# A decoder layer in float32 on one core: query projections by one level of Strassen's algorithm

## The reference

```python
q = (hidden_states @ Wq.T).reshape(bsz, q_len, H, HD).transpose(0, 2, 1, 3)
k, v = cross_attention_states @ Wk.T, cross_attention_states @ Wv.T
q, k = _rmsnorm(q, q_norm_w), _rmsnorm(k, k_norm_w)
scores = jnp.einsum('bhqd,bhkd->bhqk', q, k) / np.sqrt(HD) + attention_mask
probs = jax.nn.softmax(scores, axis=-1)
out = jnp.einsum('bhqk,bhkd->bhqd', probs, v)
return out @ Wo.T
```

## Time and profile before

| | |
|---|---|
| median of 3 runs | 1005.98 us |
| lowest, highest | 1003.19, 1006.21 us |
| the profiled execution, own time | 1007.58 us |
| its span, first to last instruction | 1005.8 us |
| mean granted TensorE clock | 0.986 of full |
| PE busy | 966.1 us (96%) |
| DVE, ACT, POOL busy | 573.8, 494.2, 404.0 us |
| HBM traffic | 43.10 MB read, 2.10 MB written |

### The profile page before, as it was taken

The page is one execution under the profiler, slowest core; times in us unless marked ns, Lnnn a source line. Parts: engine busy times, 40 slices in busy tenths (PEclk is TensorE's granted clock), DMA queues, the critical chain, the costliest instruction groups (busy, mean ns, idle before and its releaser), DMA issues.

```text
span 1005.8 us, 15353 instructions
## 1 busy us (share of the span) xinstructions
PE 966.1 (96%) x5010; PEld 804.8 (80%) x5010; DVE 573.8 (57%) x1340; ACT 494.2 (49%) x1368; POOL 404.0 (40%) x341
## 2 busy tenths in 40 slices
PE   5999799999999999899999999999999999999895
PEld 3866488878888888788888888888888888888782
DVE  3665554422321357566666666666566666666777
ACT  4655342422231246555654654654655555555554
POOL 4334634744443453342442442532622623514322
PEclk9999999999999999899999999999999999999997
DMA  6200013310111111011010020020020020100002
GB/s 218 82 3 31 12 46 125 105 63 0 63 63 63 44 62 56 22 43 43 22 54 29 21 83 0 21 83 0 21 83 0 27 78 0 63 0 0 1 1 85
DMA packets 12977, 45.60 MB, mean 45 GB/s; under 512 B 1617, under 2 KB 2257, under 8 KB 9873
## 3 DMA queue, kind: packets, MB, share of 16 engines
q1 hardware_dynamic: 12944, 45.20, 12.9%
HBM read 43.10 MB, written 2.10 MB: 45 GB/s over the span
## 4 chain that ended last, share of the span: by engine, by line
PE 86%; DVE 5%; POOL 3%; ACT 2%; issue 2%; DMA 1%; SPq 0%; POOLq 0%; DVEq 0%; ACTq 0%
PE bank L376 25%; PE bank L378 24%; PE bank L377 24%; PE bank L654 6%; PE bank L664 3%; PE bank L387 1%; POOL res L1438 1%; DVE cbuf L1638 1%; POOL rstd L1333 1%; PE bank L641 1%; DVE bst L1775 1%; POOL h_lo L1327 1%; DMA res<-in_x 1%; PE bank L455 1%; PE bank L744 0%
## 5 line engine op out<-in xcount | busy, mean ns | idle before, releaser
L376 PE MATMUL bank<-act_hi,w_hi 128*128 128x512 f32 x560 | 225.0, 402 | 2.0 <-DVE act_lo L1585 1.6
L378 PE MATMUL bank<-act_hi,w_lo 128*128 128x512 f32 x560 | 220.0, 393 | 0.0
L377 PE MATMUL bank<-act_lo,w_hi 128*128 128x512 f32 x560 | 220.0, 393 | 0.0
L1509 POOL TENSOR_TENSOR pb<-pb,prec 128x512 f32<-128x512 f32 x64 | 66.6, 1040 | 311.6 <-DVE prec L1910 311.6
L1161 ACT ACTIVATE pb<-pb,nmax 128x128 f32<-128x128 f32 x256 | 99.8, 391 | 79.1 <-DVE nmax L1905 79.1
L376 PEld LDWEIGHTS bank<-act_hi,w_hi 128*128 128x128 f32 x560 | 106.1, 189 | 25.6 <-issue 4.3
L378 PEld LDWEIGHTS bank<-act_hi,w_lo 128*128 128x128 f32 x560 | 106.1, 189 | 22.9
L377 PEld LDWEIGHTS bank<-act_lo,w_hi 128*128 128x128 f32 x560 | 106.2, 190 | 22.7 <-issue 1.4
L376 PE MATMUL bank<-w_hi,ot_hi 128*128 128x512 f32 x256 | 105.0, 410 | 0.8 <-DVE ot_lo L1585 0.8
L378 PE MATMUL bank<-w_hi,ot_lo 128*128 128x512 f32 x256 | 100.9, 394 | 0.0
L377 PE MATMUL bank<-w_lo,ot_hi 128*128 128x512 f32 x256 | 100.3, 392 | 0.0
(11 more groups left out here) (190 smaller groups left out, 2066.4 us busy)
## 6 DMA issues: line engine op xcount, KB each, us to landing
raw_a<-in_w_q SPq DMA_DIRECT2D x8, 1024.0 KB, 4.8
raw_b<-in_w_o SPq DMA_DIRECT2D x8, 1024.0 KB, 4.8
raw_a<-in_w_gu SPq DMA_DIRECT2D x7, 1024.0 KB, 5.3
raw_b<-in_w_kv SPq DMA_DIRECT2D x8, 512.0 KB, 3.3
raw_b<-in_w_dn SPq DMA_DIRECT2D x7, 512.0 KB, 3.3
res<-in_x SPq DMA_DIRECT2D x8, 256.0 KB, 6.1
raw_b<-in_ctx_t SPq DMA_DIRECT2D x8, 256.0 KB, 3.2
xre<-in_x SPq DMA_DIRECT2D x2, 1024.0 KB, 7.0
```

What stands on the lines that cost most here:

```text
L376: mm(o, l_hi, r_hi, start=first, stop=False)
L377: mm(o, l_hi, r_lo, start=False, stop=False)
L378: return mm(o, l_lo, r_hi, start=False, stop=last)
L1509: TT(pb[:, jj % 2, :, :], pb[:, jj % 2, :, :], prec[:, jj % 2, :].unsqueeze(2).to_broadcast([P, GH, L]), ALU.mult).then_inc(p_norm, 1)
```

## The change

A query projection of a group is a product of 2 by 2 blocks: weights A (two pairs of heads by two halves of the features, `quad(A11)` to `quad(A22)`, 128x512 each in `raw_a`) and activations B (halves of the features by halves of the tokens). For groups 1 to 7 it is now done with 7 block products in place of 8. Each block product (`q_prod`) is 12 matmuls of 512 columns: 2 heads by 2 feature blocks by 3 passes. Group 0 stays as it was. What it adds:

- POOL makes the sums of weight blocks for each of the groups 1 to 7 (`combine_s`, `combine_s1`, `combine_s4`: 4 operations of 128x512), and four operations on products (`combine_u4`); it splits 7 blocks (`wp_rest`) where it split 4. ACT rounds 7 (`wp_hi`) where it rounded 4.
- Once, in group 0, the sums of activation blocks T1 to T4 are made: 12 operations of 128x512 on POOL in slots (0,0) and (0,1) for T1, T2 and half of T4 (`combine_t1` 4, `combine_t2` 6, `combine_t4_head` 2), 2 more in (0,3), 6 on DVE (`combine_t3`), 8 roundings on ACT (`t_round`), 8 rests on DVE (`t_rest`).
- DVE adds the products up (`q_add`, 12 additions of 128x512 in a group, one operand in PSUM); ACT copies product 0 out (`q_copy`). `q_evac` is gone from groups 1 to 7; the squares are taken from `q_t` (`q_square`), through a single buffer `q2` in place of two.
- The order inside a slot changes on all engines. On PE the scores come ahead of the query product; slots (g,1) to (g,7) hold products 0 to 6 of group g+1 and slot (g,0) none. In (0,2) and (0,3) the product stands at the end of the slot. In (0,0) the three heads of group 0 that are left are projected at once, so group 7 has no query product in its own slots. With j < 3 DVE takes the reciprocal ahead of `add_out`.
- SP loads w_q by quarters and w_o in three pieces, some of them through `raw_a`. `ident` stays, the other constants, the LoRA weights and some buffers share memory with others; the LoRA weights are loaded after the last use of what they lie on.

The diff, cut to its core (new functions of one engine stand together):

```diff
+BLOCK_AT = [A11, A11, A12, A21, A11, A12, A22]
+PART_EARLY = {5: (1, 0, 3), 6: (1, 0, 1), 0: (0, 1, 0), 1: (0, 1, 1), 2: (0, 1, 3)}
+PART_LATE = {4: (1, 0, 2), 5: (1, 0, 0), 1: (0, 1, 2)}
...
+    def next_group(g, more=True):
+        sp_eng.wait_ge(wo_l, 4 * g + 1)
+        if not first_group(g):
+            load_quad(A21, g + 1, ld_a2)
+            sp_eng.wait_ge(wq_l, split_at(g, 6) + 1)
+            load_quad(A22, g + 1, ld_a2)
         sp_eng.wait_ge(wo_l, 4 * g + 4)
...
+        sp_eng.wait_ge(wq_l, split_at(g + 1, 2) + 1)
         sp_eng.wait_ge(wkv_l, 2 * g + 4)
+        load_quad(A12, g + 1, ld_a12)
+        load_wo(g + 1, 0, 1024, raw_b[:, 0:1024], ld_o)
+        sp_eng.wait_ge(wq_l, split_at(g + 1, 3) + 1)
...
+    def q_prod(gn, i):
+        pe.wait_ge(wq_l, split_at(gn, i) + 1)
+        if isinstance(gn, int) and gn == 1 and i in (1, 2, 3, 6):
+            pe.wait_ge(t_lo, {2: 2, 1: 4, 3: 6, 6: 8}[i])
+        if i == 0:
+            pe.wait_ge(q_ev, 8 * gn)
+            pe.wait_ge(kraw_done, 8 * gn - 2)
+        for m in range(2):
+            if 1 <= i <= 3:
+                pe.wait_ge(qc_done, 6 * gn - 6 + 2 * (i - 1) + m + 1)
+            elif i > 3:
+                pe.wait_ge(q_ev, 8 * gn + 2 * (i - 4) + m + 1)
+            for k in range(2):
+                c0 = WP_COL[i % 2] + (2 * m + k) * P
+                b_hi, b_lo = prod_rhs(i, k)
+                t = mm3(bank[m][:, :], w_hi[:, c0:c0 + P], w_lo[:, c0:c0 + P], b_hi, b_lo,
+                        k == 0, k == 1)
+            t.then_inc(q_mm, 1)
...
+        behind = first_group(g) and jj in (2, 3)
+        turn = (g, jj + 1) if j < 3 else (pg, 4 * pn)
+        if j == 3:
+            kt_step(pg, pn)
+        else:
+            kv_step(pg, pn, j + 1 if j else 0)
+            s_step(*turn)
+        if make and jj and not behind:
+            q_prod(g + 1, jj - 1)
+        if not before:
+            q_step(1, 1)
         if j == 0:
-            kv_step(pg, pn, 0)
-        if j < 3:
-            q_step(pg, pn, j + 1)
-            kv_step(pg, pn, j + 1)
-        else:
-            kt_step(pg, pn)
-            if lead:
-                q_step(g + 1, n, 0)
-        s_step(*((g, jj + 1) if j < 3 else (pg, 4 * pn)))
+            kv_step(pg, pn, 1)
+        if not before:
+            q_step(1, 2)
+            q_step(1, 3)
+        if j == 3:
+            s_step(*turn)
         pt_step(g, jj)
         if before:
             d_step(*((g, jj - 1) if jj else (g - 1, 7)))
         if j == 2:
             qs_step(pg, pn)
         pv_step(g, jj)
+        if make and behind:
+            q_prod(g + 1, jj - 1)
...
+    def wp_hi(gn, i):
+        act.wait_ge(*((ld_q, 16 * gn + 16) if i == 0 else (ld_a12, 16 * gn) if i == 5 else
+                      (ld_a2, 32 * gn) if i == 6 else (s_cmb, 8 * gn - 8 + (0, 2, 1, 3, 4)[i])))
+        act.wait_ge(q_mm, prod_at(gn, i - 2) + 2 if i >= 2 else prod_at(gn, 0) - 2 * i)
+        c0 = WP_COL[i % 2]
+        A(w_hi[:, c0:c0 + 512], quad(BLOCK_AT[i]), ACT.Copy).then_inc(wq_h, 1)
...
+    def q_square(g, n, h):
+        i = head_at(g, n, h)
+        act.wait_ge(q_ev, i + 1)
+        if not (isinstance(i, int) and i == 0):
+            act.wait_ge(qtr_done, i)
+        A(q2[:, :], q_t[:, n, h, :], ACT.Square).then_inc(qsq_done, 1)
+    def q_copy(gn):
+        for m in range(2):
+            act.wait_ge(q_mm, prod_at(gn, 0) + m + 1)
+            A(p1_s[m], bank[m][:, :], ACT.Copy).then_inc(qc_done, 1)
...
+        start = first_group(g)
+        turn = (g, jj + 1) if j < 3 else (pg, 4 * pn)
         if j == 0:
             kv_evac(pg, pn, 0)
-        if j < 3:
-            q_evac(pg, pn, j + 1)
+        if start and jj == 0:
+            softmax_exp(*turn)
+            q_evac(1, 1)
+        if jj in PART_EARLY and (make or jj < 3):
+            d, qn, qh = PART_EARLY[jj]
+            q_square(g + d, qn, qh)
+        if j == 3:
+            kt_evac(pg, pn)
+        elif j:
             kv_evac(pg, pn, j + 1)
+        if make and jj < 7 and jj != 1 and not (start and jj == 0):
+            wp_hi(g + 1, jj)
+        if j == 0:
+            kv_evac(pg, pn, 1)
+        if start and jj == 0:
+            q_evac(1, 2)
+            q_evac(1, 3)
+        pt_evac(g, jj)
+        if start and jj == 0:
+            wp_hi(1, 0)
         else:
-            kt_evac(pg, pn)
-            if lead:
-                q_evac(g + 1, n, 0)
-        pt_evac(g, jj)
-        softmax_exp(*((g, jj + 1) if j < 3 else (pg, 4 * pn)))
-        if refill and jj in WQ_SLOT:
-            for h in WQ_SLOT[jj]:
-                wq_hi(g + 1, h)
-        if jj == 0 and not (isinstance(g, int) and g == 0):
+            softmax_exp(*turn)
+        if make and jj == 1:
+            q_copy(g + 1)
+            wp_hi(g + 1, jj)
+        if jj == 0 and not start:
             for h in range(GH):
                 wo_hi(g, h)
-        if refill and jj == 2:
+        if make and jj == 2:
             wkv_hi(g + 1, 0)
             wkv_hi(g + 1, 1)
+        if start and jj in (1, 2, 4):
+            t_round(*{1: (t3, t3_raw, 6), 2: (t2, t2_raw, 10), 4: (t4, t4_raw, 14)}[jj])
         ot_evac(g, jj)
+        if start and jj == 2:
+            t_round(t1, t1_raw, 6)
+        if jj in PART_LATE and (make or jj < 3):
+            d, qn, qh = PART_LATE[jj]
+            q_square(g + d, qn, qh)
...
+    def combine_s(gn):
+        pool.wait_ge(ld_a2, 32 * gn)
+        pool.wait_ge(*((wq_l, 4) if isinstance(gn, int) and gn == 1 else (wo_l, 4 * gn - 2)))
+        TT(quad(A12), quad(A11), quad(A21), ALU.subtract).then_inc(s_cmb, 1)
+        pool.wait_ge(s_cmb, 8 * gn - 7)
+        pool.wait_ge(wq_l, split_at(gn, 0) + 1)
+        TT(quad(A11), quad(A22), quad(A12), ALU.subtract).then_inc(s_cmb, 1)
...
+        if make and jj == 1 and not first_group(g):
+            combine_s(g + 1)
+        if make and jj == 4:
+            combine_s4(g + 1)
+        if make and jj < 7 and jj != 1:
+            wp_rest(g + 1, jj)
+        if make and jj == 4:
+            combine_u4(g + 1)
+        if first_group(g) and jj == 3:
+            combine_t4()
+        if first_group(g) and jj == 0:
+            pool.wait_ge(q_mm, 4)
+            pool.wait_ge(t3_step, 4)
+            combine_t1()
         p_scale(*((g, jj + 1) if j < 3 else (pg, 4 * pn)))
         if j == 2:
             q_rsqrt(pg, pn)
-        if refill and jj in WQ_SLOT:
-            for h in WQ_SLOT[jj]:
-                wq_rest(g + 1, h)
-        if jj == 0 and not (isinstance(g, int) and g == 0):
+        if first_group(g) and jj == 0:
+            combine_t2()
+        if make and jj == 1:
+            if first_group(g):
+                combine_s(1)
+                combine_t4_head()
+            wp_rest(g + 1, 1)
+            combine_s1(g + 1)
+        if jj == 0 and not first_group(g):
             for h in range(GH):
                 wo_rest(g, h)
-        if refill and jj == 2:
+        if make and jj == 2:
             wkv_rest(g + 1, 0)
             wkv_rest(g + 1, 1)
...
+    def q_add(gn, i):
+        if i in (1, 5):
+            dve.wait_ge(s_mm, 8 * gn - 4 if i == 1 else 8 * gn)
+        if i == 4:
+            dve.wait_ge(s_cmb, 8 * gn)
+        for m in range(2):
+            dve.wait_ge(q_mm, prod_at(gn, i) + m + 1)
+            if i < 4:
+                dve.wait_ge(qc_done, 6 * gn - 6 + 2 * (i - 1) + m + 1)
+            o, first = ((q_t[:, 0, m, :], p1_s[m]), (u3_s[m], q_t[:, 0, m, :]),
+                        (q_t[:, 0, 2 + m, :], u3_s[m]), (q_t[:, 0, m, :], q_t[:, 0, m, :]),
+                        (q_t[:, 1, m, :], p1_s[m]), (q_t[:, 1, 2 + m, :], u3_s[m]))[i - 1]
+            TT(o, first, bank[m][:, :], ALU.add).then_inc(qc_done if i < 3 else q_ev, 1)
...
+        start = first_group(g)
         if j == 0:
             v_rest(pg, pn, 0)
         if not before:
-            q_part(0, 1, 0)
             softmax_rec(0, 0)
+        if j in (1, 2):
+            v_rest(pg, pn, j + 1)
+        if j == 2:
+            k_var(pg, pn)
         if j < 3:
-            q_part(pg, pn, j + 1)
-            if j == 2:
-                k_var(pg, pn)
             softmax_max(*turn)
-            pt_rest(g, jj)
-            v_rest(pg, pn, j + 1)
-            if j == 2:
-                k_norm(pg, pn)
+        if not before:
+            combine_t3()
+        if j == 0:
+            v_rest(pg, pn, 1)
+        if jj in PART_EARLY and (make or jj < 3):
+            d, qn, qh = PART_EARLY[jj]
+            q_part(g + d, qn, qh)
+        if j == 3 and make and not (start and jj == 3):
+            q_add(g + 1, jj - 1)
+        pt_rest(g, jj)
+        if j == 2:
+            k_norm(pg, pn)
+        if j < 3 and make and jj > 1 and not (start and jj < 4):
+            q_add(g + 1, jj - 1)
+        if j == 3:
+            softmax_max(*turn)
         else:
-            pt_rest(g, jj)
-            softmax_max(*turn)
-            if lead:
-                q_part(g + 1, n, 0)
+            softmax_rec(*turn)
         if before:
```

(17 more changed lines are left out.)

399 lines of the change are left out of this document (275 added, 124 removed).

## The result

The changed kernel took 1016.25 us in the median of 4 runs (1014.85 to 1016.74), beside 1006.1 (1003.19 to 1007.19) for the kernel before: a ratio of 1.0103, with a 95% interval of 1.008 to 1.0127. It is slower, by 1%. The profiled execution's own time is 1016.74 us, its span 1014.9.

What follows compares the result with a forecast made beforehand. PE bound it, busy 966.1 of 1005.8 us. +20.9 set-up, +1.0 slots (0,4) to (0,6), +2.3 clock, -14.0 six periods, -4.3 slots (7,0) to (7,2): +5.9 on 1007.58, so 1013.5, or 1011.9 on the median's scale; range 993 to 1020.

Steps and rivals of the forecast that it cites:

- The sum: Whole kernel: all terms together +5.9 us on the profiled execution's 1007.58, so 1013.5, or 1011.9 on the median's scale.
- the likeliest case: Whole kernel: slower, at 1009 to 1018 us with chance 0.46; the closing numbers give 1004 to 1018.
- The set-up: Slots (0,0) to (0,3): PE waits on queues behind POOL's activation sums; +20.9 us, 5.5 of it work moved ahead.
- the clock: Slots (0,2) and (0,3): long PE waits drop the clock to half; +2.3 us, bounds 0 and 5.
- The period: Steady part: each period 72.8 - 2.74 + 0.4 us; six of them -14.0, bounds -16.4 to -7.4.
- The wait in (g,0): Steady slot (g,0), without a product: DVE ready at 7.3 us, `pv_step` due at 6.9, so PE waits 0.4.
- (7,0) to (7,2): Last group's slots: no product covers the softmax chain, so -4.3 us of the 8.2 saved; bounds -6.5 and -2.
- the `q_rsqrt` line: POOL line named as proof: a period of 70.4 to 70.6 us read from it would show the forecast right.
- rival 3: Steady slots (g,0) and (g,2): DVE or POOL sets the pace, waits of 1.5 or more per period; about 1021 us, chance 0.12.
- Rival 1: ACT's queue in (0,1): set-up hidden if `wp_hi(1,1)` doesn't hold `ot_evac`; 17 us less, 995 us, chance 0.25.
- Rival 2: Set-up: waits of 23 us are off by 5 or so, so it cancels; 1003 to 1009 us, chance 0.17.
- Two SBUF operands: Set-up's `t_rest` on DVE taken at 1.2 us each, ends 0.68 and 1.78; skill's exclusion rule would add about 2 us.

Runs made afterwards that it cites:

- the matmuls without use: Changed kernel plus 47 matmuls whose results nobody reads, placed in PE's three long waits of slot (0,2): 1015.18 us, ratio 1.009.
- the kernel with the new order: Changed kernel with group 0's set-up reordered on POOL and DVE, and `q_part` behind `pt_rest` in slots (g,0) of groups 1 to 7: 1007.58 us, ratio 1.0018.

## Why the prediction was right, and where its parts were off

**The sum.** +5.9 was forecast against the profiled execution, +9.1 came between the spans: 3.2 more, about what a measurement of this kernel can tell. By the medians 1011.9 was forecast and 1016.25 measured, +10.2. That lies in the likeliest case, which the prediction gives once as 1009 to 1018 and once as 1004 to 1018.

**The set-up is the cause, as argued.** Forecast +20.9 for (0,0) to (0,3), +2.3 for the clock and +1.0 for (0,4) to (0,6), in all 24.2; by the marks 21.6 + 2.6 = 24.2. Without the sums of the activations 17.6 of them go (16.1 and 1.5), 5.55 are the matmuls moved ahead, forecast as 5.5, and 1.1 between (0,3) and (0,7) stay without the sums too: PE waits 0.8 us in (0,3) for the copy of the keys (forecast 0.9, in the 20.9). The moments held: POOL starts at 412.38 (forecast 412.9), the scales are ready at 420.0 and 429.1 (420.4 and 429.3), `combine_s` ends at 431.64 (431.9), `ot_lo` is done at 434.5 (435.0), product 1 starts at 448.08 (449.0). ACT idled for 7.80 us there (forecast some 7). Part of this is luck: the waits came to 18.4 us, not 23.0, and more time than forecast was lost at half clock. The longest wait was on `ot_lo` as forecast, but the second is not on `pt_lo` at `pv_step`: it is 3.8 us on `qpart` at the fold, which stands ahead of `pv_step` and needs a head's sums from the same row of DVE's steps. POOL was without idle time only to 437, not to 443: it then waits 3.00 and 2.12 us for DVE. From 434.60 to 452.76 PE's clock was at 1.2 GHz for much of the time, as the distance of 0.43 us between the starts of 512-column matmuls shows,

```profile
435.19 0.63 PE L481 MATMUL bank<-w_lo,ot_hi 128*128 128x512 f32 x1
435.62 0.63 PE L482 MATMUL bank<-w_hi,ot_lo 128*128 128x512 f32 x1
```

so that the projection took 4.6 us for 2.83 and product 1 4.68 for 2.87. Of this only product 1's share is on the path: the matmuls without use gave 1.7 us back, where I took 2.3. That the slow projection's share falls into the wait that follows it fits these numbers; it was not tested by itself.

**The period is the term of the sum that was mis-sized.** -14.0 was forecast for six, -12.1 came; a period of 70.46 was forecast, and the last ones take 70.67. PE's timeline of after, slot (g,0) and the length of slot (g,2):

```profile
644.01 0.36 PE L480 MATMUL bank<-w_hi,ctx_hi 128*128 128x256 f32 x1
...
645.51 0.60 PE L799 MATMUL bank<-cst,pb 128*128 128x128 f32 x4
...
645.87 0.48 PE L480 MATMUL bank<-w_hi,ot_hi 128*128 128x512 f32 x1
...
649.04 0.50 PE L480 MATMUL bank<-pt_hi,v_hi 128*128 128x512 f32 x1 [0.17 <-DVE pt_lo L1877]
...
658.78 0.28 PE L480 MATMUL bank<-w_hi,ctx_hi 128*128 128x256 f32 x1
...
667.99 0.60 PE L776 MATMUL bank<-cst,kraw 128*128 128x128 f32 x4
```

The wait in (g,0) was sized well: the projection and its wait take 649.04 - 645.87 = 3.17 where 2.83 is the projection, so 0.34 for the 0.4 forecast. (The prediction's own terms for DVE add up to 7.4 and not 7.3, a wait of 0.5.) (The 0.17 in brackets is less, since the end of the matmul before it is modelled.) What I had at nothing is the new order on PE. The scores now stand between two groups of another kind, and the second `kv_step` behind them takes 645.51 - 644.01 = 1.50 us, not 1.41; slot (g,2), with as many matmuls as before, takes 9.21, not 9.16; the second half of a group, from one mark to the next, takes 36.48 us, not 36.40. In all 72.80 - 2.74 + 0.34 + 0.09 + 0.05 + 0.08 = 70.62. That is 0.2 a period over the forecast, 1.2 for six, and the first two periods are another 0.7 longer (70.88 and 71.19), with one wait of 0.27 for POOL's split in the second; the rest of that stays unexplained. DVE's forecast 55.7 us came as 54.2, POOL's 42.9 as 42.7 (the stretch 845.87 to 916.54 above).

**(7,0) to (7,2)**: -4.3 forecast, -3.6 came, in the bounds. **The tail**, from (7,3) on, got 1.1 longer, which no step of mine had: the same 264 matmuls were busy for 51.48 us at a mean clock of 0.87, where before had 50.38 at 0.89. The clock differs in the first ten microseconds behind the mark of (7,3). After, then before:

```profile
949.36:959.36 10.00, 8.38 (x44) 7.29 (x42) 6.86 (x19) 4.26 (x13) 4.92 (x4) 0.83 0.00 0
```

```profile
941.39:951.39 10.00, 7.55 (x48) 6.28 (x46) 8.05 (x24) 4.38 (x13) 6.13 (x5) 1.00 0.00 0
```

The other kernels of this study sort themselves the same way: where the clock is 1.00 in these ten microseconds the tail takes 64.20 and 64.26 us (the new order, and no activation sums), in the eight others, at 0.66 to 0.83, it takes 65.6 to 66.0. Just ahead of the mark, slot (7,2) has a wait of 1.8 us at the fold that before has not, since no product covers it. All kernels with the change have that wait, and in two the clock did not fall, so it can't be the whole reason, and what decides stays open.

**The yardstick that failed.** I named the `q_rsqrt` line as proof of the period. It gives

```profile
L1757 POOL TENSOR_TENSOR qr<-qv,pow_m x15: 2899/2902/2907, 445.7 to 950.5; 128x16 f32<-128x16 f32 x15
```

504.8 / 14 = 36.06 us a half, or 72.1 a period: by my own test (over 71.5) rival 3. It is wrong because its first call lies in (0,2), ahead of product 1 and the wait for it, 7.1 us ahead of the mark of (0,3), while its last stands 1.1 us behind that of (7,3). Marks that bound only the steady slots give 70.80.

**The rivals.** Rival 1, the set-up hidden by ACT's queue alone, is refuted twice: with `ot_evac` ahead of the rounding only 3.2 of the supposed 17 us went, since DVE's queue has the next wait ready. Its time of 995 us is nevertheless where the kernel without activation sums lands (996.71), so the bound was right and the means were not. Rival 2 is what reordering gives (1007.58). Rival 3 had its place right: the spare at product 1 is about as small as laid out, since moving `q_part` made product 1 wait for POOL; it did not have its size, for no wait on `pt_lo` in the six periods was over 0.2 us.

**Two SBUF operands.** T3's rest took 3.21 us for two operations beside POOL's splits and sums of 128x512, one of which went from 1.26 to 1.72 us; 2.4 had been taken. By the Trainium skill, "SBUF — State Buffer", the section on the two separate sides, such a pair excludes each other for the whole instruction, which agrees here. But T2's rest took 1.28 for two beside POOL's `q_rsqrt`, a 128x16 operation that also reads SBUF and runs over the whole of it:

```profile
445.69 2.90 POOL L1757 TENSOR_TENSOR qr<-qv,pow_m 128x16 f32<-128x16 f32 x1 [0.16 <-DVE qv L2202]
```

That is full speed, with nobody excluded. In the kernel with the new order it is 1.28 again (438.17, `q_rsqrt` on POOL from 437.61 to 440.51), and T3's two rests took 1.76 each as soon as splits of 128x512 followed. So it does not decide here that the partner reads SBUF; whether its small size or its kind of operation does was not told apart. The measurement decides over the Trainium skill's rule.

## What to carry to other kernels

A saving per period that is certain (a matmul less) must pay for a one-time set-up, and that set-up is paid in queue order, not in engine time: here the same operations cost 21.6 us in one order of POOL's, ACT's and DVE's queues and 8.4 in another, both against the same kernel before and with the 5.5 of matmuls moved ahead in them. Look for what stands behind a wait in an in-order queue, follow it over every engine before believing that one move frees it, and compare traces by marks that stand at the same place of the work. Where a product's cover moves, say ahead of time which wait appears next: in the steady slots a wait that an edit took away came back, for the most part, as a wait on another engine.

## What the runs showed of the hardware

- PE's granted clock had means of 0.66 and 0.50 in stretches where its waits were 4.8, 3.8 and 2.7 us, with matmul starts 0.43 us apart instead of 0.23, and stayed at 1.00 there when matmuls without use filled the waits. From 411.1 to 429.8, with waits of 1.5, 1.5 and 2.6 us, it was 1.00, while before it was at 0.50 behind a wait of 1.98.
- A wait that ends at half clock costs twice: product 1 took 4.68 us, 1.8 over its full-clock time. The set-up got 1.7 shorter when all of its slow groups ran at full clock.
- DVE's subtraction with two SBUF operands is slowed beside POOL's 128x512 operations (1.6 us each) and not beside a 2.9 us `pow` of 128x16 (0.64 each).
- Kernels with the same code ahead of the attention differ by up to 2.7 us there (first mark at 390.21 to 392.89). The three with a mark at 392.3 or later (before, after, and the one with matmuls without use) have a mean granted clock of 0.76 from 118 to 132 us, the nine others 0.88. So effects under 3 us must be read from a stage.
